# Attention beside a mixture of experts: two indirect transfers in flight, expert rows loaded two experts ahead, seven batches combined by GpSimd, unread band products

## What is computed

```python
xn = _layernorm(x, axis=-1)
x = x + attention(xn) + moe(xn)

# attention, 16 heads of 8 columns
scores = jnp.einsum('bthd,bshd->bhts', q, k) * scale
attn = jax.nn.softmax(scores, axis=-1)
out = jnp.einsum('bhts,bshd->bthd', attn, v).reshape(B, T, C)
return out @ wo_w.T + wo_b

# experts: top 2 of 8, at most 1280 rows each, ranked in order of the rows
logits = xt @ gate_w
top_logits, top_idx = jax.lax.top_k(logits, k)
exp_rank = jnp.cumsum(exp_mask.reshape(k * n, E), axis=0) - 1
exp_mask = exp_mask * (exp_rank < cap).astype(jnp.int32)
h = jnp.einsum('ecd,edh->ech', exp_batches, c_fc) + fc_bias
h = jax.nn.gelu(h, approximate=False)
exp_out = jnp.einsum('ech,ehd->ecd', h, c_proj) + proj_bias
out = jnp.einsum('nec,ecd->nd', cb_weight, exp_out)
```

## Time and profile before

| | us |
|---|---|
| three runs: median (lowest to highest) | 714.14 (707.48 to 723.22) |
| the profiled execution | 716.14 |
| its span, first to last instruction | 714.3 |
| PE busy, of the span | 618.3 (87%) |
| VectorE busy | 406.7 (57%) |
| ScalarE busy | 394.9 (55%) |
| GpSimd busy | 229.0 (32%) |
| mean granted clock of TensorE | 0.880 |

### The profile page before, as it was taken

One profiled execution on the slowest core, in us unless ns is written; L12 is line 12 of the kernel. 1 busy time (PEld: TensorE's weight loads), 2 busy tenths in 40 slices (PEclk: granted clock), 3 DMA queues, 4 the chain that ended last, 5 costly groups with the idle time before them and its releaser, 6 DMA issues.

```text
span 714.3 us, 9757 instructions
## 1 busy us (share of the span) xinstructions
PE 618.3 (87%) x3526; PEld 322.6 (45%) x3526; DVE 406.7 (57%) x601; ACT 394.9 (55%) x775; POOL 229.0 (32%) x230
## 2 busy tenths in 40 slices
PE   4767999599999999989778867969999999899884
PEld 2433443223333343358767766869334333224312
DVE  5758598458888979831111110111798988857602
ACT  3442067357778877883144134323877787655751
POOL 3856911623343431200110011010255566322310
PEclk9989599759999999999789989889999999756955
DMA  6887044211212121422133033211312122111120
GB/s 191 248 277 233 21 180 155 72 38 51 73 54 74 59 68 39 119 67 74 34 107 104 27 84 108 64 45 38 102 47 76 48 73 80 58 43 27 47 66 15
DMA packets 57999, 60.44 MB, mean 85 GB/s; under 512 B 8032, under 2 KB 42848, under 8 KB 57952
## 3 DMA queue, kind: packets, MB, share of 16 engines
q1 hardware_dynamic: 52160, 45.92, 21.3%
q0 software_dynamic: 5792, 13.90, 6.3%
HBM read 29.65 MB, written 29.62 MB: 83 GB/s over the span
## 4 chain that ended last, share of the span: by engine, by line
PE 52%; DVE 21%; DMA 8%; ACT 6%; SPq 5%; issue 4%; POOL 1%; another core or an unknown queue 1%; DVEq 0%; POOLq 0%; ACTq 0%
DVE nmax L765 14%; PE bPV L983 14%; PE bX L967 12%; PE bD L1074 12%; DMA xe<-slot_x 5%; PE bD L948 5%; ACT probs L621 4%; PE bPV L1109 2%; PE bX L957 2%; DMA k_rows<-hid 2%; PE bD L991 1%; PE bD L1002 1%; DVE ye L808 1%; SPq L368 1%; DVE attn L783 1%
## 5 line engine op out<-in xcount | busy, mean ns | idle before, releaser
L765 DVE TENSOR_REDUCE nmax<-bD 128x2 f32<-128x1024 f32 x256 | 300.5, 1218 | 76.5 <-PE bD L948 58.7
L621 ACT ACTIVATE probs<-bX 128x512 f32<-128x512 f32 x512 | 268.2, 597 | 114.7 <-PE bX L967 102.6
L967 PE MATMUL bX<-Q,K 27*128 27x512 f32 x512 | 186.4, 503 | 19.0 <-ACT probs L621 12.6
L983 PE MATMUL bPV<-probs,v_aug 128*32 128x512 f32 x1024 | 152.0, 668 | 1.6 <-ACT probs L621 0.7
L967 PEld LDWEIGHTS bX<-Q,K 27*128 27x128 f32 x512 | 76.0, 196 | 163.5 <-ACT probs L621 111.3
L948 PE MATMUL bD<-K,Q 25*128 25x512 f32 x512 | 137.2, 508 | 10.7 <-DVE nmax L765 7.4
L1074 PE MATMUL bD<-wpj,hid 128*128 128x128 f32 x640 | 88.2, 306 | 11.4 <-DVE xeT_lo L798 6.3
L1074 PEld LDWEIGHTS bD<-wpj,hid 128*128 128x128 f32 x640 | 85.8, 220 | 14.8 <-issue 14.8
L512 POOL DMA_INDIRECT slot_x<-xn_all,put_i x64 | 62.4, 975 | 90.3 <-PE bPV L983 76.4
L649 ACT ACTIVATE hid<-bX,fcb 128x512 f32<-128x512 f32 (+1 forms) x96 | 55.5, 615 | 47.1 <-PE bX L1063 46.5
L948 PEld LDWEIGHTS bD<-K,Q 25*128 25x128 f32 x512 | 58.6, 197 | 47.1 <-DVE nmax L765 29.8
(11 more groups left out here) (104 smaller groups left out, 488.3 us busy)
## 6 DMA issues: line engine op xcount, KB each, us to landing
K<-k_rows SPq DMA_DIRECT2D x128, 50.0 KB
Q<-q_rows SPq DMA_DIRECT2D x128, 48.0 KB
slot_x<-hid POOLq DMA_DIRECT2D x10, 512.0 KB, 3.0
xe<-slot_x SPq DMA_DIRECT2D x8, 640.0 KB, 6.3
slot_y<-ye SPq DMA_DIRECT2D x8, 640.0 KB, 4.3
q_rows<-hid SPq DMA_DIRECT2D x8, 512.0 KB, 3.7
k_rows<-hid SPq DMA_DIRECT2D x8, 512.0 KB, 5.4
acc<-in_x SPq DMA_DIRECT2D x8, 256.0 KB, 4.9
```

Of the source, the lines that this page charges most:

```text
L621: taken(nc.scalar.activation(probs[:, (g % 2) * 4 + i, :], next_x()[:], ACT.Exp, scale=SCALE))
L765: nc.vector.tensor_reduce(nmax[q][:, k, 2 * pair:2 * pair + 2], bank()[:], AX.X, ALU.max, negate=True).then_inc(s_dd, 1)
L967: filled(nc.tensor.matmul(next_x()[:], K[u][rows_used, q, j * P:(j + 1) * P], Q[u][rows_used, q, :], start=True, stop=True))
L983: last = nc.tensor.matmul(bPV[32 * h:32 * h + 32, :], v_aug[b % 2][:, j, u * UH + QUAD * q + h, :], probs[:, (g % 2) * 4 + h, :], start=(g ...
```

## The change

- The fills of slot_x, the puts and the gathers have two semaphores each, used in turn, and the wait ahead of a transfer is for the one two before it. put_after and got_after are gone: GpSimd no longer waits for PE's groups.
- The addition of bo to acc is cut into eight pieces, one per batch, and stands between the first sixteen puts. take_out(b) waits for b + 1 pieces.
- SP loads the rows of experts 0 and 1 ahead of its loop, and in the loop those of e + 2 ahead of the wait for the results of e, once the last rows of e + 1 are transposed.
- GpSimd combines batches 0 to 6 instead of 0 to 3: 4 to 6 behind all gathers, each after take_out of its batch (taken_out). VectorE combines batch 7 alone. SP stores batches 4 to 6 after its last turn.
- In groups 8 to 15 of the last batch ahead(pair) issues two band products of queries and keys (unused_products) that nobody reads.
- keep_clock ahead of the first pair of step 2 issues eight products instead of three.

The diff, without blank lines and most of the context:

```diff
@@ -59,7 +59,7 @@
 EXPERTS_AFTER = 3
-COMBINED_BY_POOL = 4
+COMBINED_BY_POOL = 7
 N_CONST, N_LATER = 8, 3
@@ -72,17 +72,11 @@
-def put_after(i):
-    return 4 + i * (GROUPS_BEFORE - 16) // KN
-def got_after(i):
-    return GROUPS_BEFORE + 1 + i * (B * GB - GROUPS_BEFORE - 4) // KN
-COMBINED_AT = {GROUPS_BEFORE + 9 + 7 * b: b for b in range(COMBINED_BY_POOL, B - 1)}
+def taken_out(b):
+    return D_FIRST + (b + 1) * D_TURN + (E * D_EXPERT if b > EXPERTS_AFTER else 0)
@@ -245,7 +239,7 @@
         s_slots = sem("s_slots")
-        s_put = sem("s_put")
+        s_put = [sem("s_put0"), sem("s_put1")]
         s_chain = sem("s_chain")
@@ -261,9 +255,9 @@
         s_split = sem("s_split")
-        s_zero = sem("s_zero")
+        s_zero = [sem("s_zero0"), sem("s_zero1")]
         s_slot = sem("s_slot")
-        s_get = [sem(f"s_get{b}") for b in range(B)]
+        s_get = [[sem(f"s_get{b}{q}") for q in range(2)] for b in range(B)]
         s_comb_p = sem("s_comb_p")
@@ -370,12 +364,15 @@
             def experts():
-                sp.wait_ge(s_put, KN * 16)
+                for q in range(2):
+                    sp.wait_ge(s_put[q], KN // 2 * 16)
                 load_rows(0)
+                sp.wait_ge(s_dd, rows_item(0, NCH - 1) + 1)
+                load_rows(1)
                 for e in range(E):
-                    if e < E - 1:
-                        sp.wait_ge(s_dd, rows_item(e, NCH - 1) + 1)
-                        load_rows(e + 1)
+                    if e + 2 < E:
+                        sp.wait_ge(s_dd, rows_item(e + 1, NCH - 1) + 1)
+                        load_rows(e + 2)
                     sp.wait_ge(s_dd, results_end(e))
@@ -391,7 +388,7 @@
                     max_rows(1, 1, m + 1)
-                    take_pool(2, COMBINED_BY_POOL)
+                    take_pool(2, 4)
                     return
@@ -421,6 +418,7 @@
+            take_pool(4, COMBINED_BY_POOL)
             for b in range(COMBINED_BY_POOL, B):
@@ -498,20 +496,24 @@
             nc.gpsimd.memset(hid_f[:, 0:per], 0.0).then_inc(s_fill, 1)
-            pool.wait_ge(s_xn, B)
-            nc.gpsimd.tensor_tensor(acc[:], acc[:], bo_s[:, None, :].to_broadcast([P, NT, C]), ALU.add).then_inc(s_bo, 1)
             pool.wait_ge(s_fill, 7)
...
                 pool.dma_start(slot_x.rearrange("(p h r) c -> h p (r c)", p=P, h=ZERO_DMAS)[h], hid_f[:, 0:per]
-                               ).then_inc(s_zero, 16)
-                pool.wait_ge(s_zero, h * 16 + 16)
+                               ).then_inc(s_zero[h % 2], 16)
+                wait(pool, s_zero[1 - h % 2], (h + 1) // 2 * 16)
+            pool.wait_ge(s_xn, B)
+            pool.wait_ge(s_zero[(ZERO_DMAS - 1) % 2], ZERO_DMAS // 2 * 16)
             for k in range(TOPK):
...
                     col = k * NT + n
-                    pool.wait_ge(s_pv, put_after(col))
+                    wait(pool, s_put[col % 2], col // 2 * 16)
                     pool.indirect_dma_start(slot_x, bass.IndirectOffsetOnAxis(ap=put_i[:, col:col + 1], axis=0),
                                             xn_all[:, n, :], None, bounds_check=SLOTS - 1, oob_is_err=False
-                                            ).then_inc(s_put, 16)
+                                            ).then_inc(s_put[col % 2], 16)
+                    if col < 2 * B and col % 2 == 1:
+                        b = col // 2
+                        nc.gpsimd.tensor_tensor(rows(acc, b), rows(acc, b), bo_s[:, None, :].to_broadcast([P, TT, C]),
+                                                ALU.add).then_inc(s_bo, 1)
             for e in range(E):
@@ -523,8 +525,12 @@
             def combine(b):
-                pool.wait_ge(s_get[b], TOPK * TT * 16)
-                got = xn_all[:, b * TOPK * TT:(b + 1) * TOPK * TT, :].rearrange("p (k n) c -> p k n c", k=TOPK)
+                for q in range(2):
+                    pool.wait_ge(s_get[b][q], TOPK * TT // 2 * 16)
+                pool.wait_ge(s_dd, taken_out(b))
+                where = xn_all[:, :, :] if b < 4 else hid_f[:, 0:NT * C].rearrange("p (n c) -> p n c", c=C)
+                n = b % 4 * TOPK * TT
+                got = where[:, n:n + TOPK * TT, :].rearrange("p (k n) c -> p k n c", k=TOPK)
                 weights = wgt[:].rearrange("p (k n) -> p k n", k=TOPK)[:, :, b * TT:(b + 1) * TT]
@@ -538,12 +544,17 @@
                         col = k * NT + b * TT + n
-                        pool.wait_ge(s_pv, got_after((b * TOPK + k) * TT + n))
+                        if k * TT + n >= 2:
+                            pool.wait_ge(s_get[b][n % 2], (k * TT + n) // 2 * 16)
+                        elif b > 0:
+                            pool.wait_ge(s_get[b - 1][n % 2], TOPK * TT // 2 * 16)
                         pool.indirect_dma_start(gathered(b, k * TT + n), None, slot_y,
                                                 bass.IndirectOffsetOnAxis(ap=get_i[:, col:col + 1], axis=0),
-                                                bounds_check=SLOTS - 1, oob_is_err=False).then_inc(s_get[b], 16)
-                        if 0 < b <= COMBINED_BY_POOL and (k, n) == (0, 2):
+                                                bounds_check=SLOTS - 1, oob_is_err=False).then_inc(s_get[b][n % 2], 16)
+                        if 0 < b <= EXPERTS_AFTER + 1 and (k, n) == (0, 2):
                             combine(b - 1)
+            for b in range(EXPERTS_AFTER + 1, COMBINED_BY_POOL):
+                combine(b)
@@ -785,7 +796,7 @@
             def take_out(b):
-                dve.wait_ge(s_bo, 1)
+                dve.wait_ge(s_bo, b + 1)
                 take()
@@ -822,7 +833,8 @@
-                dve.wait_ge(s_get[b], TOPK * TT * 16)
+                for q in range(2):
+                    dve.wait_ge(s_get[b][q], TOPK * TT // 2 * 16)
                 dve.wait_ge(s_dd, d.value())
@@ -844,8 +856,6 @@
                     normalise(0)
-                if b * GB + g in COMBINED_AT:
-                    combine(COMBINED_AT[b * GB + g])
@@ -911,6 +921,7 @@
             d = Count()
+            hot_f = hot[:].rearrange("p n e -> p (n e)")
@@ -948,6 +959,13 @@
+            def unused_products():
+                to = free()
+                for n in range(2):
+                    at = STRIP * n
+                    nc.tensor.matmul(to[:, n, :], Q[1][at:at + NR_MAX, 1, 0:P], K[1][at:at + NR_MAX, 1, :], start=True, stop=True)
@@ -1016,6 +1034,8 @@
                         scores_for_max(b + 1, 0, head - GB, pair)
+                    else:
+                        unused_products()
@@ -1099,7 +1119,6 @@
             pe.wait_ge(s_hot, 1)
-            hot_f = hot[:].rearrange("p n e -> p (n e)")
             nc.tensor.matmul(bX[1][:], prefix_r[:], hot_f, start=True, stop=True)
@@ -1113,7 +1132,7 @@
                     if s >= 2:
-                        keep_clock(3)
+                        keep_clock(8 if (s, pair) == (2, 0) else 3)
                     scores_for_max(0, 0, s, pair)
...
                     maxima(0, 0)
```

## The result

| | before | after |
|---|---|---|
| runs side by side: median (lowest to highest), us | 713.08 (707.48 to 723.22), 4 runs | 645.27 (635.83 to 648.11), 4 runs |
| ratio, 95% interval | | 0.8993 [0.8832, 0.9153] |
| the profiled execution, its span, us | 716.14, 714.3 | 635.83, 634.0 |
| PE, VectorE, ScalarE, GpSimd busy, us | 618.3, 406.7, 394.9, 229.0 | 568.5, 400.5, 393.1, 244.6 |
| mean granted clock | 0.880 | 0.982 |

The change makes the kernel faster by 10%. The ratio in this table leaves out executions over 1.5% above a kernel's fastest, while all medians, and the ratios of medians further down, are over all executions, because what sets them apart is the clock, which is the subject. The profiled execution is the fastest of its four. The others took 643.29, 648.11 and 647.26 us at mean clocks of 0.967, 0.954 and 0.958.

A forecast was written before the change was run, and what follows sets the result against it. No one engine bounds throughout; time is lost where PE idles and the clock drops. Gains of 6 + 36.4 + 15.4 + 10.2 = 68.0 us, and 2.0 for the profiled execution, taken from 716.1 give 646 us; range 622 to 682.

The forecast's parts named there:

- The forecast: Whole kernel: one common stall stays, all other gains come as summed, 646 us; chance 0.47.
- the second case: Whole kernel: the common stall goes as well, 15.8 us more gained, 630 us; chance 0.25.
- the third case: Clock still drops in the lead, the batch from 596 to 658 us or the end: 652 to 669 us; chance 0.18.
- The experts: Expert stage: rows loaded earlier end PE's waits and the low clock behind them; gain 36.4 us, lower bound 30.
- The combinations: Batch from 596 to 658 us: moving VectorE's combinations to GpSimd gains 15.4 us, or 2.3 if the clock falls otherwise.
- The lead: 68 to 88 us, before group 0: five more unread products hold the clock; gain 6 us, bounds 0 and 8.5.
- the nmT rows: Rows the first scores wait for: there just in time at 84.5 us, 2.5 us taken off for busy DMA engines.
- The step on the clock: Lead: PE's 1.99 us wait drops the clock; five more products leave 0.5 to 0.9 us idle, so it holds.
- The end: Last eight groups: unread band products keep PE busy and the clock up; gain 10.2 us, 0 if not.
- The stall: 131 to 160 us: PE, ScalarE and VectorE stop together during a long put series; costs 15.8 us, not plainly removed.
- The puts: GpSimd's 64 puts, two in flight, at worst one every 1.5 us, end near 195 to 205 us; nothing gained.
- The batches: Undisturbed attention batches take 47.3 us between output adds; the range's low end allows 5 us for losses beside them.

The follow-up runs named there:

- e9: The kernel after, unchanged, measured again: median 660.88 us, 0.922 of before.
- e4: The kernel after with VectorE instead of GpSimd combining batches 4 to 6: median 656.11 us, 0.917 of before.
- e2: The kernel after without the unread band products in groups 8 to 15 of the last batch: median 662.64 us, 0.926 of before.
- e1: The kernel after with expert rows again loaded late, behind the store of results and the weights: median 694.21 us, 0.970 of before.
- e3: The kernel after with three unread products instead of eight ahead of the first pair of step 2: median 641.15 us, 0.896 of before.
- e6: The kernel before, unchanged, profiled once more: 716.42 us in one run.
- e7: The kernel before with the pacing of its puts (put_after) removed: median 718.84 us, 1.012 of before.
- i2: Second measurement of the kernel after with four unread 128x512 products added in group 0 of the first batch: median 649.38 us, 0.906 of before.
- e5: The kernel after without the limit of two puts or gathers in flight: median 646.02 us, 0.909 of before.
- e8: The kernel before with only the early loading of expert rows: median 678.50 us, 0.946 of before.

## Why the prediction was right, and where its working was not

- **The number.** 646 against 645.27, but by two errors that cancel, which is luck. The forecast kept a stall of 15.8 us that no profile with the edits to GpSimd has, and had no fall at 88 us, of 14 to 17, that four of the seven profiles with its lead and nothing added in group 0 have. The profiled execution without it took 636, between the forecast and the second case's 630. Measured again (e9), the same kernel took 660.88, the third case's figure; and by the number of traces that case, "the clock is not held", describes most executions better than the forecast does. It put the failure into the lead, the batch or the end. It came right behind the lead and at the end.
- **The experts.** Right: 36.4 forecast, 35.9 in the stage, 36.8 undone, 36.6 in the stage alone (38.4 by the medians). Expert periods of 19.43, load 12 us ahead, no wait.
- **The combinations.** Right: 15.4 forecast and found, 15.3 in e4. One detail was wrong: GpSimd's three do not each follow their output add. They wait for the gathers, the last of which is issued at 587.25, and come in one go from 588.27 to 602.4, still 31 us before the end. And the argument that nothing is lost beside them was wrong. The maxima read PSUM, but the two small operations behind them work in SBUF, and beside GpSimd's products and additions they take up to 2.71 us instead of 0.18 (e2). The trace of before has it too: in the very batch of 47.32 us that the prediction cites, the cast at 594.90 takes 0.51, and the one at 535.19, a batch earlier, 0.88. In the profile of the kernel after it costs nothing that the stages show; in e1, e2 and e9 it made PE wait and the clock fall. No term of the sum stands for it.
- **The lead.** The size was right at the upper bound (8.7, 9.4 by e3, against 6 and at most 8.5), and the nmT rows were in time: SP issued them from 78.89 on, PE went into group 0 at 84.40 without a wait. The 2.5 us taken off for busy DMA engines were not due. The step on the clock was half right. The prediction had it fall by the wait of 1.99 us, and so it stands in before, e6 and e7. In eight other profiles it fell ahead of that wait, and the eight products (six of these) shortened the fall from 24 us to some 3.4. In e4, e9 and i2 it didn't fall, with 0.82 to 0.91 us of the wait left, as forecast.
- **The clock behind the lead.** The step that failed. The sum treats each stage's clock as its own: if the lead is at the higher clock, group 0 goes on at it. The runs show that a stage which arrives fast can lose the clock in the next one, at 88 to 91 us in four of seven profiles, so that e3 with its slow lead ends no later than the kernel after. Why it falls there stays open.
- **The end.** The size was right where the clock held (9.0, and 9.2 between e2 and after), but it held in four of nine profiles, and that the products are what held it isn't proven. 10.2 was counted as sure in the forecast.
- **The stall.** Whether the change removes it stays open. The price was right (15.6), and a dense series is not enough to cause the stall (e5, e6, e7). But the stall is in two of three profiles with the old GpSimd code and in none of the ten with the new, so the change may well have removed it, in a way that no run shows. The prediction leaned on one coincidence for the case it gave most weight.
- **The puts.** 1.58 us apart, just over the worst case of 1.5, and not "about what that series had", 1.28; the last at 208.81 instead of 195 to 205. Off the path, as forecast.
- **The batches.** Batch 1 took 50.84 and not 47.3, with a short fall of the clock near 168. That lies within the 5 us that the range had kept for what batches lose.

## What to carry to other kernels

A wait of PE of one or two microseconds is to be priced with the low clock that can follow it: 1.50 us cost 15.3 here, and 21.5 us of waits cost 36. A load queued behind a store that waits for results is worth moving first. Work moved to GpSimd can hold up small operations of VectorE in SBUF beside it, so look at their durations in the trace, and at what waits for them. A gain of clock in one stage counts only once a trace of several executions shows what the next stage does with it, so profile such a change more than once, and judge it by a median and not by the best execution.

## What the runs showed of the hardware

- TensorE's clock fell to 1.2 GHz behind 6 us with the engine busy for 5.71 (e9, at 88 us), and stayed there with it busy 32.73 of 34 us (e9), 69.12 of 71 us (e7) and 30.00 of 30 us (e9, end). Busy time as the profile counts it was in these stretches not enough to bring it back. In the lead, with a fall at 65 to 67 us, it was back after some 3.4 us where eight 128x512 products stood (six profiles), and after 24 us where three did (e3, e8).
- The same program with the same data had the fall at 88 us in one execution (e9) and not in another (after), with PE's busy time the same in the 6 us ahead of it (5.71 us in both).
- VectorE's operations of 128x16 elements in SBUF (nmhl) take 0.18 us, and beside a 128x512 product or addition of GpSimd up to 2.71 (e2); the reductions of the maxima out of PSUM show no such stretch (mean 1217 ns after, 1218 before).
- 64 puts 1.28 to 1.30 us apart (e5, e7) came with no common stall, and the batches behind the first took 47.3 us in both.
- A load of 640 KB took 6.4 us to land when it was issued behind a store of the same size and four loads of weights (e1), and 4.6 when it was issued ahead of them (after, e8).
